# Expert stages: the two rows of routing weights of a pair fetched by one indirect DMA from GpSimd instead of two broadcasts from SyncE

## The chip, the cores and the metric

One core of a Trainium2 chip runs the whole program. The metric is the device time of one execution in microseconds (us); lower is better. The engines are named as the profile names them: PE (TensorE), PEld (its weight loads), DVE (VectorE), ACT (ScalarE), POOL (GpSimd), SP (SyncE). A name with a q (SPq, POOLq) is the sequencer of that engine, which also issues DMAs.

## What is computed

A transformer of two layers on x of shape (2, 1024, 128), each with an attention and a mixture-of-experts block:

```python
x = x + attn_a(layernorm(x))      # 16 heads, all positions
x = x + ffn(layernorm(x))
x = x + attn_b(layernorm(x))      # 16 heads, a window of 32 positions
x = x + ffn(layernorm(x))
# ffn, for T = 2048 tokens of 128 channels, 64 experts of 64 hidden channels:
shared = silu(x @ sg_w.T) * (x @ su_w.T) @ sd_w.T
scores = sigmoid(x @ gate_w.T) + gate_bias
# the best 4 of 8 groups of experts, in them the best 6 experts; their scores normalised to sum 1
comb   = weights (T, 64), zero for the experts not chosen
h      = silu(x @ eg_w) * (x @ eu_w)            # for every expert
routed = einsum('eti,ehi,te->th', h, ed_w, comb)
```

## The kernel before

**Stages.** The program runs in five parts: a start, attention a (`attend_full`), the first expert stage (`experts`, tag M1ex, some 421 to 706 us in the trace), attention b (`attend_banded`), the second expert stage (tag M2ex, some 861 to 1139 us). Between parts stands a barrier over all engines (`end_of_layer`, L65).

**An expert stage.** All 64 experts are computed for all tokens, and the routing weights switch the unwanted ones off. The shared expert counts as two more, so there are 66, in 33 pairs (`PAIRS`); a pair fills the 128 partitions, 64 hidden channels each. The 2048 tokens are two batches of 1024, and a batch is two chunks of 512 columns. The loop counter q runs over 132 steps (`QN`): batch, then pair, then chunk; p = q // 2 counts the pairs of both batches (0 to 65). One step q is:

- PE, `gate_up(q)`: three matmuls of 128x512 into the gate bank and three into the up bank (the inputs are cut in high and low halves of 16 bits, hence three), L1829 to L1836;
- ACT, `silu(q)` (L1886) from PSUM to `sil`;
- DVE, `times_up(q)` (L1930), then `times_weight(q)` (L1940), which multiplies with the row of routing weights in `cb` and writes `hid`, a ring of 3;
- ACT, `high_part(q)` (L1892): the upper 16 bits, `high`;
- POOL, the subtraction that gives `low` (L1993), also a ring of 3. It waits for `high_ready` q+1 and for `down_done` q-2 (the down product of step q-3 is through);
- PE, `down(q)`: three matmuls (L1845, L1846, L1848), issued `LAG` = 3 steps later, behind `gate_up(q+3)`. The third reads `low`.

`times_weight(q)` waits for `low_ready` q-2, since the subtraction of step q-3 reads the same `hid` buffer.

**Work beside.** In the first batch's steps the engines also take one small slice per step of the output projection, norm and routing of the second batch (`before()` in each engine's block); from step 74 on, in the first stage, the norm and the projections of the next attention (`after()`). POOL's share of these is small: a power for the norm (L1393), the subtraction for `xl` (L1499) and one product of the routing (L1505).

**The rings and the queues.** `cb` has 5 buffers (`CB_RING`) of 128x1024 f32: partitions 0 to 63 hold the weights of the pair's first expert for all 1024 tokens of the batch, partitions 64 to 127 those of the second. They come from `comb` in DRAM, 66 rows by 2048 tokens. Pair 0 is the shared expert, filled by a DVE copy (L1961). `wt`, the six matrices of a pair, has 6 buffers. SP issues everything in program order: in each turn p it waits until `cb`'s buffer is free (`hid_ready` of pair p-5), issues the two broadcasts of pair p (`weights`, L1784, 64 partitions each, all read from one row of 4 KB), then waits for `down_done` of pair p-6 and loads the matrices (L1736). In turn 33 it first stores the second batch's `comb` (`store_weights`, L1490), and `weights(33)` waits until that has landed (`comb_stored[1]`). In the first stage turn 52 also issues the eight stores of the next attention's queries and keys (L1670); in the second, SP stores the output.

## Time and profile before

| | us |
|---|---|
| median of 3 runs | 1148.68 |
| lowest, highest | 1146.83, 1162.83 |
| span of the profiled execution | 1143.3 |
| PE busy in it | 1044.1 (91%) |
| DVE busy | 925.3 (81%) |
| ACT busy | 709.0 (62%) |
| POOL busy | 461.7 (40%) |

The span reaches from the first to the last instruction of the profiled execution. No separate time of that execution is given; its span is 5.4 us below the median of the three timed runs, and what lies around the span (launch and end) is taken as those 5.4 us. Busy times leave out waiting and the issuing of DMAs, so a DMA issued by POOL would not appear in POOL's 40%. Matmuls overlap in their pipeline, and the duration of one (some 380 ns) is longer than its share of PE's time.

### The profile page before, as it was taken

Reading aid. Unit: us, or ns where it says so; the run is one execution under the profiler, and the core shown is the slowest. Engines: PE = TensorE matmul, PEld = TensorE weight load, DVE = VectorE, ACT = ScalarE, POOL = GpSimd, SP = SyncE. Lnnn points to the kernel's source line nnn. Section 1 sums busy time; section 2 is a strip of 40 time slices with the busy share of each in tenths; the row PEclk is TensorE's granted clock in tenths of the full one; section 3 lists DMA queues with packets and bytes.
Section 4 is the critical chain, followed back from the end, with each engine's and each line's share of the span. In section 5 each row is a group of like instructions: output and inputs, shape, how many; then the busy total and the mean of one; then the engine's idle time right before and its main releaser. Section 6 shows DMA issues by size and latency. Waiting matters only on the chain. (4 is left out here: it accounts for less than half of the span.)

```text
span 1143.3 us, 18866 instructions
## 1 busy us (share of the span) xinstructions
PE 1044.1 (91%) x6314; PEld 427.5 (37%) x6314; DVE 925.3 (81%) x2139; ACT 709.0 (62%) x1089; POOL 461.7 (40%) x434
## 2 busy tenths in 40 slices
PE   5769999999999979999999998888888999999998
PEld 4212222222222325444444443334444444444443
DVE  8688999999998467889788776877876779877775
ACT  2537778777787765666666664355465566666664
POOL 4116336532100105565564554100113556556554
PEclk9758999999999989999999999679999999999999
DMA  6901302311200126566764873142206667687662
GB/s 207 253 2 28 81 9 72 80 53 28 54 2 1 43 59 170 163 170 174 196 181 140 218 193 81 34 110 59 72 4 172 157 152 188 171 208 193 182 189 57
DMA packets 72185, 131.63 MB, mean 115 GB/s; under 512 B 12680, under 2 KB 47624, under 8 KB 72088
## 3 DMA queue, kind: packets, MB, share of 16 engines
q1 hardware_dynamic: 68704, 120.92, 40.5%
q10 hardware_dynamic: 3384, 9.51, 3.1%
q8 instruction: 50, 0.82, 0.3%
q14 instruction: 47, 0.39, 0.1%
HBM read 115.08 MB, written 14.91 MB: 114 GB/s over the span
## 5 line engine op out<-in xcount | busy, mean ns | idle before, releaser
L421 ACT ACTIVATE Aatt_prob<-Aatt_st 128x1024 f32<-128x1024 f32 x256 | 247.7, 1022 | 66.1 <-PE Aatt_st L315 65.1
L487 DVE TENSOR_REDUCE Aatt_mx<-Aatt_sc 128x1 f32<-128x512 f32 x439 | 273.3, 683 | 10.0 <-PE Aatt_sc L302 9.5
L1993 POOL TENSOR_TENSOR M1ex_low<-M1ex_hid,M1ex_high 128x512 f16<-128x512 f32 x132 | 152.8, 1157 | 136.2 <-ACT M1ex_high L1892 70.1
L1993 POOL TENSOR_TENSOR M2ex_low<-M2ex_hid,M2ex_high 128x512 f16<-128x512 f32 x132 | 152.7, 1157 | 130.8 <-PE M2ex_acc L1848 73.3
L302 PE MATMUL Aatt_sc<-ks,qs 48*128 48x512 bf16 x496 | 152.5, 408 | 29.5 <-DVE Aatt_mx L487 11.8
L1886 ACT ACTIVATE M2ex_sil<-M2ex_ring,unscale 128x512 f32<-128x512 f32 x132 | 90.7, 687 | 95.3 <-PE M2ex_ring L1831 95.1
L1886 ACT ACTIVATE M1ex_sil<-M1ex_ring,unscale 128x512 f32<-128x512 f32 x132 | 90.7, 687 | 89.4 <-PE M1ex_ring L1831 88.9
L327 PE MATMUL Aatt_pv<-Aatt_prob,vg 128*32 128x512 f32 x1024 | 137.9, 611 | 0.6 <-ACT Aatt_prob L421 0.6
L1930 DVE SCALAR_TENSOR_TENSOR M2ex_ring<-M2ex_ring,unscale,M2ex_sil 128x512 f32<-128x512 f32 x132 | 100.0, 757 | 42.0 <-ACT M2ex_sil L1886 38.9
L1930 DVE SCALAR_TENSOR_TENSOR M1ex_ring<-M1ex_ring,unscale,M1ex_sil 128x512 f32<-128x512 f32 x132 | 99.9, 757 | 36.2 <-ACT M1ex_sil L1886 32.9
L302 PEld LDWEIGHTS Aatt_sc<-ks,qs 48*128 48x128 bf16 x496 | 35.9, 94 | 201.1 <-DVE Aatt_mx L487 167.7
L315 PE MATMUL Aatt_st<-qs,ks 51*128 51x512 bf16 x512 | 105.2, 387 | 4.0 <-ACT Aatt_prob L421 2.6
L1940 DVE TENSOR_TENSOR M1ex_hid<-M1ex_ring,M1ex_cb 128x512 f32<-128x512 f32 x132 | 91.3, 692 | 16.2 <-DVE M1ex_ring L1930 0.9
L1940 DVE TENSOR_TENSOR M2ex_hid<-M2ex_ring,M2ex_cb 128x512 f32<-128x512 f32 x132 | 91.3, 692 | 15.9 <-DVE M2ex_ring L1930 0.5
L828 DVE CUSTOM_DVE_ANT_0 Batt_sc<-Batt_sc,mask 128x160 f32<-128x160 f32 (+1 forms) x256 | 75.2, 347 | 25.5 <-PE Batt_sc L658 24.1
L1892 ACT CAST M1ex_high<-M1ex_hid 128x512 f16<-128x512 f32 x132 | 80.6, 610 | 17.9 <-DVE M1ex_hid L1940 15.9
L1892 ACT CAST M2ex_high<-M2ex_hid 128x512 f16<-128x512 f32 x132 | 80.5, 610 | 12.1 <-DVE M2ex_hid L1940 10.4
L787 ACT ACTIVATE Batt_prob<-Batt_st 128x320 f32<-128x320 f32 x128 | 51.1, 436 | 55.3 <-PE Batt_st L728 54.9
L1829 PE MATMUL M1ex_ring<-M_xh,M_wt 128*128 128x512 f16 x132 | 50.5, 383 | 11.0 <-DVE M1ex_hid L1940 5.4
L248 POOL CAST Aatt_mparts<-Aatt_m 128x32 bf16<-128x32 f32 x8 | 2.6, 325 | 140.1 <-DVE Aatt_m L500 140.1
L1829 PE MATMUL M2ex_ring<-M_xh,M_wt 128*128 128x512 f16 x132 | 50.4, 382 | 5.7 <-DVE M2ex_hid L1940 3.4
L1848 PE MATMUL M2ex_acc<-M2ex_low,M_wt 128*128 128x512 f16 x132 | 50.3, 381 | 1.0 <-POOL M2ex_low L1993 1.0
(437 smaller groups left out, 1959.5 us busy)
## 6 DMA issues: line engine op xcount, KB each, us to landing
M1ex_cb<-comb SPq DMA_DIRECT2D x130, 256.0 KB, 4.1
M2ex_cb<-comb SPq DMA_DIRECT2D x130, 256.0 KB, 4.2
M_wt<-wsplit SPq DMA_DIRECT2D x132, 192.0 KB, 4.0
wsplit<-split_cut SPq DMA_DIRECT2D x9, 704.0 KB, 4.5
qs<-stack SPq DMA_DIRECT2D x32, 96.0 KB
ks<-stack SPq DMA_DIRECT2D x30, 96.0 KB
split_raw<-in_wg_dram ACTq DMA_DIRECT2D x3, 704.0 KB, 8.5
split_raw<-in_wu_dram ACTq DMA_DIRECT2D x3, 704.0 KB, 12.0
```

The lines of the kernel that those rows point to most:

```text
L302: mm = pe.matmul(sc_bank(n, i), queries, ks[k][rows, jp, h * CH:(h + 1) * CH], start=True, stop=kind != "excess")
L315: mm = pe.matmul(st[jp][:, half, :], ks[k][rows, jp, kc * P:(kc + 1) * P], qs[k][rows, jp, qh * CH:(qh + 1) * CH], start=True, stop=True)
L327: mm = pe.matmul(pv[32 * j:32 * j + 32, :], vg[k][:, kc, j, :], prob[(2 * s + j % PAIR) % 4][:, j // PAIR, :], start=kc == 0, stop=kc == T ...
L421: act.activation(prob[e % 4][:, :, :].rearrange("p a c -> p (a c)"), st[pr][:, :, :].rearrange("p a c -> p (a c)"), ACT.Exp, scale=SCALE). ...
L487: ins = dve.tensor_reduce(mx[k][:, m, h:h + 1], scores, AX.X, ALU.max)
L828: ins = dve.tensor_tensor_reduce(scores, scores, mask_q[:, first:BAND], -1.0, -BARRED, ALU.add, ALU.min, accum_out=m1[k][:, j, qt:qt + 1])
L1829: pe.matmul(gate(q)[:, :], wt[k][:, 0, :], env.xh[:, cs], start=True, stop=False)
L1886: act.activation(sil[q % 2][:, :], gate(q)[:, :], ACT.Silu, scale=env.unscale[:, 0:1]).then_inc(sil_ready, 1)
L1892: act.copy(high[q % 3][:, :], hid[q % 3][:, :]).then_inc(high_ready, 1)
L1930: dve.scalar_tensor_tensor(up(q)[:, :], up(q)[:, :], env.unscale[:, 1:2], sil[q % 2][:, :], ALU.mult, ALU.mult).then_inc(up_ready, 1)
L1940: dve.tensor_tensor(hid[q % 3][:, :], up(q)[:, :], cb[k][:, c * CH:(c + 1) * CH], ALU.mult).then_inc(hid_ready, 1)
L1993: pool.tensor_tensor(low[q % 3][:, :], hid[q % 3][:, :], high[q % 3][:, :], ALU.subtract).then_inc(low_ready, 1)
```

## The change

The broadcasts leave SP's program. POOL issues, for each pair, one indirect DMA that writes all 128 partitions of the `cb` buffer: a small table `which` of 128x33 integers, made by two `iota` instructions in the start part, says for partition k and pair j which row of `comb` goes there (2j for the lower 64 partitions, 2j+1 for the upper). The table is read as offsets by the DMA. Four of them (pairs 1 to 4) are issued ahead of POOL's loop, the others one in every second step: in step q (odd) for pair q // 2 + 4, ahead of that step's subtraction. Pair 33 is thus issued in step 59, and waits there for `comb_stored[1]`. `comb` becomes two DRAM tensors, one for each batch. One DMA raises the semaphore by 16 where two raised it by 32.

```diff
             pool.wait_ge(made, 14)
+            for e in range(2):
+                pool.iota(env.which[HALF * e:HALF * e + HALF, :], [[2, PAIRS]], base=e, channel_multiplier=0).then_inc(made, 1)
+            pool.wait_ge(made, 16)
             rest_of(norm_of_batch_gpsimd(pool, env, second))
...
         @block.sync
         def _(sp):
-            def weights(p):
-
-                j, b = p % PAIRS, p // PAIRS
-                if j == 0:
-                    sp.wait_ge(env.comb_stored[b], 32)
-                for e in range(2):
-                    sp.dma_start(cb[p % CB_RING][64 * e:64 * e + 64, :],
-                                 env.comb2[j, e:e + 1, b * S:(b + 1) * S].to_broadcast([64, S])).then_inc(cb_in[p % CB_RING], 16)
-
...
-            sp.wait_ge(env.comb_stored[0], 32)
-            for p in range(1, CB_RING):
-                weights(p)
             for p in range(CB_RING, B * PAIRS):
                 sp.wait_ge(hid_ready, 2 * (p - CB_RING) + 2)
                 if p == PAIRS:
                     store_weights(sp, env, q1, 1)
-                weights(p)
                 if p >= WT_RING:
...
                 if c == 0 and p:
-                    dve.wait_ge(cb_in[k], 32 * (p // CB_RING + (k > 0)))
+                    dve.wait_ge(cb_in[k], 16 * (p // CB_RING + (k > 0)))
...
+            def weights(p):
+
+                if p % PAIRS == 0:
+                    pool.wait_ge(env.comb_stored[p // PAIRS], 32)
+                if p >= CB_RING:
+                    pool.wait_ge(hid_ready, 2 * (p - CB_RING) + 2)
+                pool.indirect_dma_start(cb[p % CB_RING][:, :], None, env.comb_rows[p // PAIRS][:, :], bass.IndirectOffsetOnAxis(
+                    ap=env.which[:, p % PAIRS:p % PAIRS + 1].bitcast(U32), axis=0)).then_inc(cb_in[p % CB_RING], 16)
+
             beside, behind = before(), after()
+            pool.wait_ge(env.comb_stored[0], 32)
+            for p in range(1, CB_RING):
+                weights(p)
             for q in range(QN):
+                if q % 2 and CB_RING <= q // 2 + CB_RING - 1 < B * PAIRS:
+                    weights(q // 2 + CB_RING - 1)
                 pool.wait_ge(high_ready, q + 1)
                 if q >= 3:
                     pool.wait_ge(down_done, q - 2)
...
-        env.comb_rows = nc.dram_tensor("comb", [ROWS, B * S], F32).ap()
-        env.comb2 = env.comb_rows.rearrange("(j e) t -> j e t", e=2)
+        env.comb_rows = [nc.dram_tensor(f"comb{b}", [ROWS, S], F32).ap() for b in range(B)]
+        env.which = sb("which_row", [P, PAIRS], I32)
```

## Rows read from the trace of the kernel before

**Rows 1.** The page, busy time of each engine, share of span, instructions.
```profile
PE 1044.1 (91%) x6314; PEld 427.5 (37%) x6314; DVE 925.3 (81%) x2139; ACT 709.0 (62%) x1089; POOL 461.7 (40%) x434
```
**Rows 2.** Windows: stretch, length, busy PE, PEld, DVE, ACT, POOL, clock, DMA share, GB/s.
```profile
430.00:706.00 276.00, 269.60 (x1287) 127.50 (x1284) 219.75 (x391) 170.59 (x284) 158.22 (x136) 1.00 0.67 173
870.00:1139.00 269.00, 265.00 (x1259) 124.25 (x1257) 208.41 (x353) 163.64 (x273) 155.91 (x135) 0.99 0.64 167
...
1000.00:1050.00 50.00, 50.00 (x237) 23.21 (x236) 37.84 (x53) 31.75 (x53) 29.45 (x26) 1.00 0.81 202
```
**Rows 3.** Waits, 421 to 706 us: us in total, times, longest.
```profile
POOL M1ex_low L1993 <- ACT M1ex_high L1892: 70.1, 52, 18.1
POOL M1ex_low L1993 <- PE M1ex_acc L1848: 65.1, 75, 2.1
...
PEld M1ex_ring L1829 <- issue: 11.8, 10, 5.5
PEld M1ex_ring L1829 <- DVE M1ex_hid L1940: 6.4, 10, 2.5
```
**Rows 4.** The page, costliest groups: shapes, count, busy, mean ns, idle before.
```profile
L1993 POOL TENSOR_TENSOR M2ex_low<-M2ex_hid,M2ex_high 128x512 f16<-128x512 f32 x132 | 152.7, 1157 | 130.8 <-PE M2ex_acc L1848 73.3
...
L1930 DVE SCALAR_TENSOR_TENSOR M2ex_ring<-M2ex_ring,unscale,M2ex_sil 128x512 f32<-128x512 f32 x132 | 100.0, 757 | 42.0 <-ACT M2ex_sil L1886 38.9
...
L1940 DVE TENSOR_TENSOR M2ex_hid<-M2ex_ring,M2ex_cb 128x512 f32<-128x512 f32 x132 | 91.3, 692 | 15.9 <-DVE M2ex_ring L1930 0.5
```
**Rows 5.** Timeline, 550 to 557 us (steps 57 to 60): start, duration, instruction, idle before.
```profile
550.55 0.38 PE L1848 MATMUL M1ex_acc<-M1ex_low,M_wt 128*128 128x512 f16 x1
550.94 1.15 POOL L1993 TENSOR_TENSOR M1ex_low<-M1ex_hid,M1ex_high 128x512 f16<-128x512 f32 x1 [0.78 <-PE M1ex_acc L1848]
...
552.72 1.09 SPq L1784 DMA_DIRECT2D M1ex_cb<-comb  x2
552.89 1.16 POOL L1993 TENSOR_TENSOR M1ex_low<-M1ex_hid,M1ex_high 128x512 f16<-128x512 f32 x1 [0.79 <-PE M1ex_acc L1848]
...
554.83 1.16 POOL L1993 TENSOR_TENSOR M1ex_low<-M1ex_hid,M1ex_high 128x512 f16<-128x512 f32 x1 [0.79 <-PE M1ex_acc L1848]
555.17 0.69 DVE L1940 TENSOR_TENSOR M1ex_hid<-M1ex_ring,M1ex_cb 128x512 f32<-128x512 f32 x1
...
556.38 0.38 PE L1848 MATMUL M1ex_acc<-M1ex_low,M_wt 128*128 128x512 f16 x1
```
**Rows 6.** DMA issues on SP by line: issue ns min/median/max; time to landing of L1784.
```profile
L1784 SPq DMA_DIRECT2D M1ex_cb<-comb x130: 444/596/1578, 421.7 to 685.1; - x130
DMA to landing us min/median/max: 3.3/4.1/7.8
...
L1736 SPq DMA_DIRECT2D M_wt<-wsplit x132: 325/584/1316, 373.5 to 1117.0; - x132
```
**Rows 7.** Timeline of the second expert stage's first 11 us.
```profile
860.84 11.43 SPq L1784 DMA_DIRECT2D M2ex_cb<-comb  x11
860.89 0.69 DVE L1961 COPY M2ex_cb<-unscale 128x1024 f32<-128x1024 f32 x1 [7.23 <-PEq L69]
...
866.63 1.16 POOL L1993 TENSOR_TENSOR M2ex_low<-M2ex_hid,M2ex_high 128x512 f16<-128x512 f32 x1 [17.98 <-ACT M2ex_high L1892]
...
869.38 0.69 DVE L1940 TENSOR_TENSOR M2ex_hid<-M2ex_ring,M2ex_cb 128x512 f32<-128x512 f32 x1
```
**Rows 8.** Timeline of DVE: the norm beside the second expert stage.
```profile
911.65 0.17 DVE L1367 TENSOR_TENSOR M2exln_r<-M2exln_r 128x8 f32<-128x8 f32 x1 [1.75 <-POOL M2exln_r L1393]
```
**Rows 9.** Timeline of POOL in the start part.
```profile
10.47 1.95 POOL L983 TENSOR_SCALAR_AFFINE_SELECT mask<-mask 128x320 bf16<-128x320 bf16 x4
...
13.34 0.13 POOL L997 MEMSET fresh_g<- 128x8 bf16 x1
25.88 1.64 POOL L1393 TENSOR_TENSOR startln_r<-startln_ve,minus_half 128x8 f32<-128x8 f32 x1 [12.41 <-DVE startln_ve L1363]
```
**Rows 10.** POOL's groups by line: its only library instruction.
```profile
L1091 POOL PARTITION_ALL_REDUCE split_alltop<-split_top x1 | 0.4, 420 | 5.7 <-issue 5.7
```

More of the change, by code:

```diff
@@ L1489, in store_weights @@
         sp.wait_ge(q.comb_copied, c + 1)
-        sp.dma_start(env.comb_rows[:, b * S + c * CH:b * S + (c + 1) * CH],
+        sp.dma_start(env.comb_rows[b][:, c * CH:(c + 1) * CH],
                      q.combT[:, c * CH:(c + 1) * CH]).then_inc(env.comb_stored[b], 16)
```

## The prediction

> **What bounds the kernel now.** I read the page first: PE is busy 91% of the span, POOL 40% [rows 1]. Since the change touches the two expert stages, the average says little, and I cut those stages into windows. From 1000 to 1050 us PE is busy 50.00 of 50 us; over both stages without their first microseconds it is busy 269.6 of 276 and 265.0 of 269 [rows 2]. So PE sets the pace there, and any transfer or engine that is not later than PE is free. The timeline of four steps gives the pace: the third down matmul of step 54 starts at 550.55, that of step 57, three steps on, at 556.38, so 5.83 / 3 = 1.94 us a step, 3.89 us a pair [rows 5]. Next I asked whether anything waits for what is taken out. The waits of the stage have no line in which DVE waits for `cb`; POOL's own waits, 70 and 65 us, are for ACT and for the down matmuls [rows 3]. The broadcasts land 4.1 us after issue (7.8 at most) [rows 6], and are issued four pairs, some 15 us, ahead. What the change removes is thus hidden already, and the question is what it adds to POOL.
>
> **POOL's room.** A subtraction takes 1.157 us [rows 4], two of them in a pair 2.31 us. In a pair of 3.89 us that leaves 1.57 us, if PE sets the pace. Averaged over both stages: 545 us of window less 158.2 + 155.9 us of busy POOL is 230.9 us, and 61 issues fall in each stage's loop (pairs 5 to 65), so 230.9 / 122 = 1.89 us for each [rows 2]. The mean is higher since some steps carry more side work; that surplus can't be moved to other pairs, because the rings hold only three steps. So the limit for POOL's cost D of one indirect DMA lies at 1.57 us in the dense stretches and 1.89 us over all.
>
> Within that limit the delay itself must be harmless too. In step 59 the DMA would go out when the subtraction of step 58 is over, 552.89 + 1.16 = 554.05. The subtraction of step 59 starts at 554.83 now, so it comes D - 0.78 us late [rows 5]. Who waits for it: the down matmul of its own step, and DVE's write of `hid` three steps later. For the first, `low` of step 57 is done at 552.09 and read at 556.38: 4.3 us of room. For the second, DVE writes `hid` of step 60 at 555.17: 3.1 us of room. A D of up to 0.78 + 3.1 = 3.9 us would pass as a single delay; only the sum over a pair, 1.57 us, binds.
>
> **The part without a row: D.** The trace has no DMA issued by POOL. From below: SP's generator is held 0.58 us by the matrices' load, a 128-partition transfer [rows 6], and POOL's one library instruction is shown with 0.42 us [rows 10]. A software generator isn't likely to beat the first, and I exclude a gain, because POOL issued nothing of the kind before; the low end is 0.4 us. From above: 5.7 us of idle before that library instruction, for which the profile shows no reason [rows 10], and 4.1 us, if POOL were held until the data are there [rows 6]. Between those ends the nearest row is the same work on the other engine: the two broadcasts of a pair, together 128 rows of 4 KB, hold SPq 1.09 us [rows 5]. I take that, D = 1.1 us, with a likely spread of 0.6 to 2.3 us, twice the row. At 1.1 us POOL needs 3.41 of 3.89 us: the steady state costs nothing, and what hides it is PE's pace.
>
> The Trainium skill, on its page "SBUF — State Buffer" (section "A bandwidth-pool intuition that's wrong"), has a rule that speaks against the change: a DMA issued by GpSimd has its descriptors written by that engine through a port that VectorE locks in its two-port modes, and one that takes some 620 ns alone took some 3100 ns beside such a copy. By 3.1 us for each, the sum would be 122 x (3.1 - 1.57) = 187 us. The trace speaks against it here: DVE's two large operations of every step read `ring`, a PSUM bank [rows 4], and POOL's subtraction next to them has a mean of 1157 ns, no instance of it stretched enough to move that mean. The one large copy from SBUF to SBUF, 0.69 us, stands at the stage's start [rows 7], exactly where the first four DMAs go: at most 0.7 us, and covered as below.
>
> **The other edits.** *Four DMAs ahead of the loop.* POOL sits idle for 17.98 us before its first subtraction at 866.63, and the barrier ends at 860.84, when SP starts: 5.8 us for four DMAs, 4.4 us at my D. If that cover is gone (D above 1.45) the first subtraction is late, with over 3 us of room to its readers. DVE first needs `cb` of pair 1 at 869.38; issued at 860.84, it is there at 860.84 + 1.1 + 4.1 = 866.0 [rows 6, 7]. Nothing. *The wait in step 59.* SP's own wait for the stored rows ended at 552.72, when it issued the next broadcast; POOL reaches the wait at 554.05, 1.3 us later [rows 5]. Behind that wait stands the subtraction of step 59, and if the store were late it has 3.1 us more. Nothing, twice. *The wait for `hid_ready`* in each step asks for q - 1, and the subtraction before it already needed step q - 1 finished: no wait. *The norms beside the loop.* DVE waits 1.75 us for POOL's power [rows 8], and PE for DVE up to 2.5 us [rows 3], so here POOL is on the path, three times in the program (two norms in the first stage, one in the second). The DMA stands ahead of the subtraction ahead of the power and makes it D - 0.78 = 0.3 us late: 3 x 0.3 = 1 us; at D = 2.2 it would be 4 us. *The two `iota`.* They write 64x33 integers; four operations of 320 columns take 1.95 us, and POOL idles 12.41 us right behind them [rows 9]. Nothing. *SP* loses 130 issues of 0.6 us in each stage [rows 6] and waits instead. The matrices are issued up to 1 us earlier, with a ring of six pairs ahead: nothing, unless the rival below holds. *DMA traffic* stays 512 KB a pair for `cb`; the engines are 64 to 67% busy [rows 2].
>
> **Sum.** Profiled span 1143.3 + 0 (loop) + 1 (norms) = 1144.3; with the 5.4 us between span and median, 1149.7, say 1150 us.
>
> **Rivals.** *POOL becomes the bound (slower).* The mechanism is D itself: above 1.57 us each pair takes 2.31 + D. At D = 2.2, twice SPq's row, that is 0.6 us a pair. Over 122 pairs at most 74 us, at least (2.2 - 1.89) x 122 = 38 us; I take 60, with the norms' 4 some 1210 us. For it: the offsets must be fetched before a descriptor can be made, and the profile shows how close 1.57 us is to 1.1. Against: only that SPq's row is the nearest. It decides 2% (23 us) from D of about 1.8 us. A far case of the same mechanism, D = 4.1, gives (4.1 - 1.57) x 122 = 309 us, some 1450 us; 4.1 us is a transfer's whole time to landing, which an issuing engine need not sit through, and SPq doesn't.
> *The matrices come sooner (faster).* PE idles with no visible reason before L1829 in the first stage, 11.8 us, 5.5 of them at its start [rows 3]. If the rest of it were a matrix load queued behind broadcasts, the change would give some 6 us back there and as much in the other stage: 1138 us. Against it: loads are issued six pairs ahead.
> *The change doesn't do what it says:* the rows of 4 KB are cut in smaller pieces by the software generator. Then there are more descriptors in a DMA, D grows, and it ends as the slow case.
>
> **How the numbers follow.** A measurement of this kernel can tell some 2% (23 us) from no change. Forecast, D up to 1.8 us: 0.55. POOL the bound, D 1.8 to about 2.6, or cut rows: 0.34. The far case: 0.07. Matrices sooner: 0.04, half of which I allow to pass 2%. So faster 0.02, same 0.57, slower 0.41. The likeliest case's own range is 1140 to 1172. The range must reach into the slow case: up to D = 2.3, (2.3 - 1.57) x 115 = 84 us, 1235; above that lies about 0.13, below 1138 some 0.04.
>
> **What would show it.** Right: in the windows of the expert stages PE stays above 97% busy; POOL's subtraction waits for PE or ACT in the even steps as now, and in the odd steps follows the DMA with no idle time named; no DVE wait for `cb`. Wrong: pairs of more than 3.89 us in 1000 to 1050 us, POOL's subtractions back to back with the DMA (D read off as the gap between the end of an even subtraction and the start of the odd one), PE and DVE waiting for `low`. A D above 1.57 us makes the prediction wrong, and only that can by much.

## The result and the profile after

| | before | after |
|---|---|---|
| median, us | 1149.42 | 1165.47 |
| lowest, highest | 1144.94, 1164.63 | 1153.66, 1169.74 |
| executions | 18 | 18 |

The medians differ by 16 us (1.4%). The estimated ratio is 1.0114, with a 95% interval of 1.0083 to 1.0144 (this estimate, and not the quotient of the medians, stands in the tables below). By the bound of 2% that is no change, but the interval leaves out 1: the kernel is slower, by 16 us in the median where 1 was forecast. The forecast of 1150 us was 15 us too low, inside its range of 1138 to 1235.

The 18 times after the change lie in two groups, 7 from 1153.7 to 1158.2 and 11 from 1164.6 to 1169.7, and the groups differ in the mean clock that PE was granted (0.943 to 0.947 against 0.925 to 0.932). The profiled execution is one of the upper group: 1166.2 us, span 1164.4, so 1.8 us lie around the span. The profile of before has a span of 1143.3 and a clock of 0.948, like its fastest executions. A comparison of the two profiles therefore holds two things at once, and the experiments had to part them.

The page after the change, busy time and the DMA queue (its columns: packets, MB, share of 16 engines):

```profile
PE 1061.5 (91%) x6314; PEld 433.0 (37%) x6314; DVE 933.1 (80%) x2139; ACT 710.8 (61%) x1089; POOL 593.5 (51%) x566
...
q0 software_dynamic: 18720, 68.17, 16.2%
...
L1997 POOL TENSOR_TENSOR M2ex_low<-M2ex_hid,M2ex_high 128x512 f16<-128x512 f32 x132 | 153.9, 1166 | 44.6 <-ACT M2ex_high L1882 32.7
...
L1984 POOL DMA_INDIRECT M2ex_cb<-comb,which_row x65 | 63.9, 983 | 24.1 <-POOLq L69 14.2
L1984 POOL DMA_INDIRECT M1ex_cb<-comb,which_row x65 | 64.9, 999 | 21.8 <-POOLq L69 11.8
```

Against [rows 1] POOL has 132 more instructions, 130 DMAs and two `iota`, and goes from 40% to 51%. Its other work has not stretched: 1166 ns for a subtraction against 1157 [rows 4]. An indirect DMA is shown as work of the engine (POOL, not POOLq), and so does count in POOL's busy share, other than the section on the time before says. It takes 0.98 to 1.00 us in the mean. The queue's 18720 packets are 130 x (128 + 16), and 128 x 130 rows of 4 KB make 68.16 MB: the rows went out whole, so the prediction's third rival, rows cut in smaller pieces, did not occur.

The windows of the expert stages, with the columns of [rows 2]; the fourth is attention b:

```profile
430.00:712.00 282.00, 273.31 (x1295) 128.52 (x1293) 223.09 (x393) 171.76 (x285) 219.70 (x197) 0.99 0.51 170
885.00:1160.00 275.00, 268.82 (x1278) 125.41 (x1276) 215.01 (x362) 168.03 (x278) 219.32 (x198) 1.00 0.49 168
...
1020.00:1070.00 50.00, 50.00 (x237) 23.22 (x236) 37.89 (x54) 31.31 (x53) 41.48 (x39) 1.00 0.58 192
...
716.00:884.00 168.00, 145.81 (x1356) 69.58 (x1357) 116.10 (x653) 74.15 (x180) 19.90 (x48) 0.73 0.19 52
```

In the dense stretch PE is still busy 50.00 of 50 us, and POOL 41.48 instead of 29.45. How a pair looks there, in the timeline of POOL:

```profile
1042.38 1.16 POOL L1997 TENSOR_TENSOR M2ex_low<-M2ex_hid,M2ex_high 128x512 f16<-128x512 f32 x1 [1.22 <-PE M2ex_acc L1838]
1043.68 0.96 POOL L1984 DMA_INDIRECT M2ex_cb<-comb,which_row  x1
1044.65 1.17 POOL L1997 TENSOR_TENSOR M2ex_low<-M2ex_hid,M2ex_high 128x512 f16<-128x512 f32 x1
...
1046.26 1.16 POOL L1997 TENSOR_TENSOR M2ex_low<-M2ex_hid,M2ex_high 128x512 f16<-128x512 f32 x1 [0.44 <-ACT M2ex_high L1882]
```

One subtraction ends at 1042.38 + 1.16 = 1043.54 and the next starts at 1044.65: the DMA costs POOL 1.11 us, gap included. The subtractions ahead of it and behind it still have idle time before them, 1.22 and 0.44 us, in which POOL waits for PE and ACT. POOL is not the bound.

So where are the 21.1 us of span? I cut both traces at DVE's writes of `hid` (steps 0, 66 and 131 of each stage) and at POOL's first copy for attention b, the first thing after the first stage's barrier. The same cut was made for each experiment, and one table serves them all. "Barrier" runs from the last `hid` to that copy; "attention b" from there to the first `hid` of the second stage (so it is longer than the 137 us that the expectations give for it), "tail" from the last `hid` to the end; the last two columns are the clock granted in attention b and the whole span. All in us, the clock as a share of full speed:

| kernel | M1 to 66 | M1 | barrier | attention b | M2 to 66 | M2 | tail | clock | span |
|---|---|---|---|---|---|---|---|---|---|
| before | 141.30 | 277.81 | 6.69 | 154.68 | 143.14 | 269.87 | 8.76 | 0.86 | 1143.3 |
| after | 145.79 | 281.61 | 9.15 | 167.57 | 144.67 | 271.41 | 9.02 | 0.73 | 1164.4 |
| first_only | 144.52 | 280.34 | 9.14 | 156.82 | 143.13 | 269.87 | 8.76 | 0.85 | 1150.9 |
| second_only | 142.73 | 279.24 | 6.83 | 158.39 | 145.60 | 272.33 | 9.03 | 0.84 | 1151.0 |
| onedma | 141.36 | 277.89 | 6.85 | 154.54 | 143.17 | 269.90 | 8.76 | 0.86 | 1144.2 |
| latebarrier | 142.72 | 279.24 | 9.60 | 161.19 | 143.15 | 269.88 | 8.76 | 0.80 | 1154.3 |
| noload | 141.15 | 277.61 | 6.69 | 168.97 | 141.89 | 268.66 | 8.75 | 0.73 | 1155.9 |
| behind | 142.44 | 280.88 | 9.15 | 163.14 | 143.17 | 269.90 | 9.02 | 0.79 | 1157.4 |
| halves | 165.84 | 322.07 | 6.39 | 156.70 | 166.09 | 316.08 | 8.75 | 0.85 | 1236.4 |
| plain_two | 146.03 | 281.93 | 6.38 | 166.04 | 146.33 | 273.07 | 8.74 | 0.76 | 1162.1 |
| second_batch | 142.70 | 278.51 | 6.59 | 163.64 | 141.69 | 268.43 | 8.80 | 0.75 | 1152.8 |
| filled | 144.58 | 280.39 | 9.53 | 156.51 | 145.60 | 272.34 | 9.02 | 0.86 | 1153.8 |
| twice | 141.53 | 278.05 | 6.68 | 161.25 | 143.12 | 269.86 | 8.76 | 0.92 | 1150.8 |
| after_twice | 144.54 | 280.36 | 9.15 | 160.67 | 144.57 | 271.31 | 9.02 | 0.91 | 1156.4 |

The first two lines differ by 3.8 us in the first stage, 2.5 at its barrier, 12.9 in attention b, 1.5 in the second stage and 0.3 behind it, 21.0 together. The second batch of each stage (M1 less "M1 to 66": 136.5 before, 135.8 after; 126.7 in both in the second stage) costs nothing. Whatever the change costs, it costs in the first batch, at the barrier and, most of all, in a stage that the diff does not touch.

**The barrier.** The drain of POOL's queue at the end of each stage (issue ns min/median/max), after; [rows 1 to 10] have no such row, so that of before follows:

```profile
L1752 POOLq DRAIN  x2: 6583/6586/6590, 708.7 to 1156.8; - x2
```
```profile
L1749 POOLq DRAIN  x2: 1256/1256/1256, 704.8 to 1136.0; - x2
```

And the timeline behind it, in the kernel after:

```profile
711.77 0.69 DVE L1937 TENSOR_TENSOR x_res<-x_res,M1ex_side 128x512 f32<-128x512 f32 x1 [0.31 <-PE M1ex_side L1843]
...
716.38 0.40 POOL L612 COPY vg<-vn 128x256 f32<-128x256 f32 x1 [6.52 <-POOLq L69]
...
716.88 0.40 PE L658 MATMUL Batt_sc<-ks,qs 48*128 48x128 bf16 x4 [5.14 <-DVEq L804]
```

DVE, the last worker of the stage, is through at 712.46, and POOL's drain at 708.7 + 6.59 = 715.3. The next stage starts 3.9 us behind DVE; before, DVE's last instruction ended at 708.58 and the copy came at 710.03, 1.45 us behind. At the end of the program SP's store of the output covers nearly all of the same drain, which leaves 0.3 us.

**The first batch.** The norm's wait came as forecast in two of its three places: DVE waits 2.13 and 2.12 us for POOL's power there, against 1.76 and 1.75 before. At the third, the next attention's norm, it waits 2.06 against 2.02. But DVE shows more than that. The routing of the second batch, in the kernel after (timeline of DVE and POOL):

```profile
529.74 1.17 POOL L1997 TENSOR_TENSOR M1ex_low<-M1ex_hid,M1ex_high 128x512 f16<-128x512 f32 x1
530.30 1.89 DVE L1552 TENSOR_TENSOR M1exrt_experts_eq<-M1exrt_masked,M1exrt_experts_top 128x256 bf16<-128x256 f32 x1
530.85 1.05 POOL L1508 TENSOR_TENSOR M1exrt_weighted<-M1exrt_masked,M1exrt_inv 128x512 f32<-128x512 f32 x1
...
533.57 0.42 DVE L1552 TENSOR_TENSOR M1exrt_experts_eq<-M1exrt_masked,M1exrt_experts_top 128x256 bf16<-128x256 f32 x1
```

The same DVE instruction takes 0.42 us alone and 1.89 us when it starts during a POOL instruction: it ends at 532.19, behind the end of the second of two POOL instructions that follow without a gap (531.90). DVE's next write of `hid` comes 3.28 us after the last instead of 1.86. The kernel before pays in this place too, but less: its two comparisons take 0.48 and 1.04 us. So the change doesn't bring these meetings, it makes them longer. The addition to the routing scores is hit too (the groups by line, after, then before):

```profile
L1572 DVE SCALAR_TENSOR_TENSOR M1exrt_sc<-M1exrt_sc,gate_b x1: 1577/1577/1577, 496.9 to 496.9; 128x512 f32<-128x512 f32 x1
```
```profile
L1569 DVE SCALAR_TENSOR_TENSOR M1exrt_sc<-M1exrt_sc,gate_b x1: 810/810/810, 495.1 to 495.1; 128x512 f32<-128x512 f32 x1
```

The Trainium skill has this on its page "SBUF — State Buffer" (section "Who interferes with whom"): a VectorE instruction with two inputs from SBUF and a GpSimd instruction that reads SBUF contend for a port that is an exclusive lock and not a share of bandwidth. The trace agrees, with 0.42 us become 1.89, and adds that one wait can last over two GpSimd instructions. The large DVE operations of each step read `ring` in PSUM [rows 4] and are not touched: 757 and 692 ns, as before.

**Attention b.** The stage takes 12.9 us longer, at a clock of 0.73 instead of 0.86. The window of before that answers to the fourth one above:

```profile
711.00:865.00 154.00, 130.09 (x1357) 62.09 (x1358) 115.72 (x653) 74.03 (x180) 16.76 (x44) 0.86 0.22 58
```

The number of matmuls is the same (1357, 1356), their busy time 130 and 146 us. The granted clock has two levels, 1.2 and 2.4 GHz, and 0.73 is a mean over stretches at either. In every kernel profiled the clock falls to 1.2 GHz in or shortly behind the stretch at the barrier in which PE stands idle (707.85 to 710.53 us before, 711.74 to 716.88 after), and stays there for 27.3 us before and 23.9 us after. So the first low stretch is not what became longer. Up to the next barrier the kernel before has one more, of 13.7 us, and the kernel after three, of 17.1, 17.1 and 27.3 us, the last two from 800.8 and 834.9 us on. The diff changes nothing in this stage.

### The profile page after: what moved, and what is told of

Read it like the earlier page. It is cut to its first block and busy times, and to the rows that moved or that the text cites. A ratio compares the mean times of both kernels' runs of the same rounds, so it can differ in the third digit from the quotient of the medians.

```text
span 1164.4 us, 18861 instructions
## 1 busy us (share of the span) xinstructions
PE 1061.5 (91%) x6314; PEld 433.0 (37%) x6314; DVE 933.1 (80%) x2139; ACT 710.8 (61%) x1089; POOL 593.5 (51%) x566
## 3 DMA queue, kind: packets, MB, share of 16 engines
q0 software_dynamic: 18720, 68.17, 16.2%
## 5 line engine op out<-in xcount | busy, mean ns | idle before, releaser
L1997 POOL TENSOR_TENSOR M2ex_low<-M2ex_hid,M2ex_high 128x512 f16<-128x512 f32 x132 | 153.9, 1166 | 44.6 <-ACT M2ex_high L1882 32.7
L1984 POOL DMA_INDIRECT M2ex_cb<-comb,which_row x65 | 63.9, 983 | 24.1 <-POOLq L69 14.2
L1984 POOL DMA_INDIRECT M1ex_cb<-comb,which_row x65 | 64.9, 999 | 21.8 <-POOLq L69 11.8
## 6 DMA issues: line engine op xcount, KB each, us to landing
split_raw<-in_wu_dram ACTq DMA_DIRECT2D x3, 704.0 KB, 13.7
```

The lines of the kernel that those rows point to most:

```text
L1984: pool.indirect_dma_start(cb[p % CB_RING][:, :], None, env.comb_rows[p // PAIRS][:, :], bass.IndirectOffsetOnAxis(ap=env.which[:, p % PAIR ...
L1997: pool.tensor_tensor(low[q % 3][:, :], hid[q % 3][:, :], high[q % 3][:, :], ALU.subtract).then_inc(low_ready, 1)
```

## The experiments

**1. Which stage, and is it the number of DMAs?** Four kernels. `first_only` and `second_only` are the changed kernel with the DMAs on POOL in one expert stage and SP's broadcasts in the other:

```diff
+        by_pool = not last          # second_only: by_pool = last
...
+                if not by_pool:
+                    weights(p)                  # SP, the two broadcasts
...
-                    dve.wait_ge(cb_in[k], 16 * (p // CB_RING + (k > 0)))
+                    dve.wait_ge(cb_in[k], (16 if by_pool else 32) * (p // CB_RING + (k > 0)))
...
-                if q % 2 and CB_RING <= q // 2 + CB_RING - 1 < B * PAIRS:
+                if by_pool and q % 2 and CB_RING <= q // 2 + CB_RING - 1 < B * PAIRS:
```

`onedma` is the kernel before with one small DMA issued by POOL in each expert stage, for a drain that has something to drain:

```diff
             beside, behind = before(), after()
+            pool.dma_start(tiny[:, :], env.sources["gate"]).then_inc(tiny_in, 16)
```

`latebarrier` is the kernel before with six fills of a `cb` buffer behind POOL's last subtraction of the first stage, so that POOL comes late to the barrier without any DMA:

```diff
+            if not last:
+                for i in range(6):
+                    if i == CB_RING:
+                        pool.wait_ge(idle_set, CB_RING)
+                    pool.memset(cb[i % CB_RING][:, :], 0.0).then_inc(idle_set, 1)
```

> The first expert stage as in the changed kernel, the second as before. Theory A (the loss is local: some 4 us inside the first stage's first batch, some 2.5 us at the barrier behind it, because POOL's drain takes 6.6 us instead of 1.3; attention b's lower clock in the profiled run is drawn by each execution, not caused): profile shows the first stage and the barrier as in the changed kernel, second stage as before, and the fastest runs lie 6 to 7 us above the fastest of before. Theory B (attention b runs at a lower clock because the stage ahead of it used POOL's DMAs): attention b again takes 150 us or more instead of 137, in most executions, and the median lies 15 us or more above before. Theory C (the DMA queue of POOL itself costs something everywhere, stores and loads of other stages included): other stages longer too.

> The second expert stage as in the changed kernel, the first as before. Theory A: 2 us above before (1.5 us inside the stage's first batch, 0.3 us at its end, where SyncE's store of the output covers most of the longer drain). Theory B: the same, since attention b stands ahead of the POOL DMAs; its clock must be that of before. If attention b is slow here too, B falls and the clock is drawn whatever the change.

> The kernel before, and in each expert stage POOL issues one small plain DMA (a 128x64 tile, read by nobody) at the stage's start. If the longer drain of POOL is a fixed price of having used its DMA queue in a block, it is 6.6 us here as well and the barrier behind the first stage comes 2.5 us later: 2.5 to 3 us above before. If it grows with the number of DMAs (69 in a stage), it is near 1.3 us and the time is that of before.

> The kernel before, with six memsets of 128x1024 on POOL (some 0.9 us each) behind its last subtraction of the first stage, so that the barrier comes some 2.5 us later without any POOL DMA. Theory A: 2 to 3 us above before, attention b as before. Theory B in its form 'the later barrier, with PE idle for 5.4 instead of 2.9 us, sends attention b into the lower clock': 10 us or more above before in the median, with attention b at a mean granted clock of 0.75 to 0.8 instead of 0.9.

| kernel | median | lowest, highest (n) | ratio to before, 95% |
|---|---|---|---|
| first_only | 1163.03 | 1152.08, 1165.36 (6) | 1.0122, 1.0081 to 1.0162 |
| second_only | 1151.54 | 1148.60, 1156.23 (12) | 1.0027, 1.0000 to 1.0055 |
| onedma | 1146.61 | 1145.54, 1153.73 (12) | 0.9995, 0.9975 to 1.0015 |
| latebarrier | 1156.05 | 1151.17, 1165.18 (10) | 1.0062, 1.0031 to 1.0094 |

The DMAs of the first stage alone bring as large a loss as the whole change (1.0122 against 1.0114); those of the second alone bring some 3 us (1.0027). `first_only` falls in two groups as the kernel after does (two times at 1152, four from 1161.9 to 1165.4), and its profile is of the lower one: with attention b at 0.85 it has all of the first stage's loss and only 2 of the 12.9 us. Both theories of its expectation are borne out in part: the lowest times lie 8 us above those of before (A forecast 6 to 7), and the median 15.7 us (B: 15 or more). One DMA in a stage (against 65 in the kernel after; the 69 of the expectation was a miscount) costs nothing, and its drain is 1.20 us:

```profile
L1749 POOLq DRAIN  x2: 1197/1200/1202, 705.7 to 1137.0; - x2
```

So the longer drain is not the price of using POOL's queue at all.

`latebarrier` delayed the barrier by 2.9 us (9.60 against 6.69) and cost more than that, 7 us at its lowest (1151.17 against 1144.29) and 8.7 in the median, between the 2 to 3 and the 10 or more of its two theories, with five of its ten times at 1156 to 1157. Of the 11.0 us in its profile 2.9 are the barrier, 1.4 the steps 22 to 26 told of below and 6.5 attention b at a clock of 0.80. A later start of attention b alone can thus go with time beyond the delay itself, but does not produce the upper group in most executions.

The table also shows a second thing that comes and goes. Steps 22 to 26 of a stage take 7.6 us in some profiles (M1 of before, of `first_only` and of `twice`; M2 of `noload` and of the kernel after) and 9.1 or 9.2 in others (M1 of the kernel after and of `second_only`; M2 of before and of `first_only`), with or without POOL's DMAs. What happens there in the longer case, in the windows of the kernel after:

```profile
474.00:478.00 4.00, 1.97 (x6) 0.79 (x7) 3.69 (x9) 1.31 (x2) 2.32 (x3) 0.81 0.41 154
478.00:482.00 4.00, 4.00 (x15) 1.62 (x14) 3.23 (x7) 1.81 (x3) 2.32 (x3) 0.76 0.19 43
```

PE is busy 1.97 of 4 us beside the norm, and the granted clock falls to 0.81 and 0.76, means over one stretch of 3.4 us at 1.2 GHz. What decides it is open: in the same place of before PE is busy 2.31 of 4 us and the clock stays at 1.00. A profile that has this carries 1.2 to 1.5 us more at step 66. Between profiles that agree in it, the DMAs cost 144.52 - 141.30 = 3.2 us up to step 66 of the first stage (`first_only` against before), of which 0.7 come back by step 84, and 144.67 - 141.89 = 2.8 us in the second (after against `noload`). The 3.8 and 1.5 us of the profiled pair are thus 2.5 + 1.3 and 2.7 - 1.2. Other pairs that agree in it give 2.4 us for the first stage (after against `second_only`) and 2.5 (`second_only` against before) to 3.0 (after against `second_batch`) for the second.

Where the loss arises shows step by step. In the second stage of `second_only` against that of before, DVE's write of `hid` falls back by 0.4 us at step 21 (the norm), 0.8 at step 31 (the addition to the scores, 1.57 us instead of 0.81), 0.35 at steps 35 and 36 (the comparisons of the groups), 0.3 at step 41 (the masking of the scores, 0.95 instead of 0.68), and 0.8 at steps 47 and 48 (the two comparisons above, 1.90 and 0.42 instead of 0.49 and 1.04). With rounding and 0.1 us won back at step 24 that is the 2.5 us. All but the norm are DVE instructions that read SBUF alone, the addition, the masking and the two comparisons with two inputs.

**2. Was the removed work worth anything, and does the place of the DMA matter?** `noload` is the kernel before with the broadcasts of 61 pairs in each stage left out, the first four pairs' kept, so DVE multiplies with old rows; neither SP nor POOL issues them:

```diff
                 if p == PAIRS:
                     store_weights(sp, env, q1, 1)
-                weights(p)
+                if p == PAIRS:
+                    sp.wait_ge(env.comb_stored[1], 32)
...
-                if c == 0 and p:
+                if c == 0 and 0 < p < CB_RING:
```

`behind` is the kernel after with the DMA moved behind the subtraction and the side work of its step:

```diff
             for q in range(QN):
-                if q % 2 and CB_RING <= q // 2 + CB_RING - 1 < B * PAIRS:
-                    weights(q // 2 + CB_RING - 1)
...
                 if q >= AFTER:
                     next(behind, None)
+                if q % 2 and CB_RING <= q // 2 + CB_RING - 1 < B * PAIRS:
+                    weights(q // 2 + CB_RING - 1)
```

`halves` cuts each indirect DMA in two, of 128 rows of 2 KB each, for the left and right 512 tokens: twice the instructions and rows, the same bytes. `plain_two` issues SP's two broadcasts from POOL, 64 partitions each, without offsets:

```diff
-                pool.indirect_dma_start(cb[p % CB_RING][:, :], None, env.comb_rows[p // PAIRS][:, :], ...
+                # halves
+                for c in range(2):
+                    pool.indirect_dma_start(cb[p % CB_RING][:, c * CH:(c + 1) * CH], None,
+                        env.comb_rows[p // PAIRS].rearrange("r (c t) -> (r c) t", c=2), ...
...
+                # plain_two
+                for e in range(2):
+                    pool.dma_start(cb[p % CB_RING][64 * e:64 * e + 64, :],
+                        env.comb_rows[b][2 * j + e:2 * j + e + 1, :].to_broadcast([64, S])).then_inc(cb_in[p % CB_RING], 16)
```

> The kernel before, with no transfer of routing weights behind pair 4: cb keeps the rows of the first pairs, so the experts are weighted wrongly; 61 pairs of broadcasts are left out in each stage, and nothing takes their place. It tells what the removed part was worth. Forecast of the prediction: nothing, within 3 us of before, since no engine waited for it. Rival (the matrices come sooner): 6 us or more faster for each stage.

> The changed kernel with the indirect DMA of an odd step issued behind that step's subtraction and side work instead of ahead. If the loss inside the first batch comes from the subtraction and the norm's power being late (0.4 us at the norm, then a lower clock of PE), it is gone or smaller here: 3 to 5 us faster than the changed kernel. If it comes from VectorE's operations on two SBUF tiles meeting POOL at work (1.3 us around step 47 in each stage), it stays about as it is, at other operations.

> The changed kernel with two indirect DMAs a pair, each of 128 rows of 2 KB (one for each half of the tokens), so the same bytes, twice the descriptors and instructions. POOL needs 2.31 + 2 x 1.27 = 4.85 us a pair where PE gives 3.89. If D is per instruction or per descriptor (0.96 us for 128 rows): POOL becomes the bound, up to 0.96 us more for each of 122 pairs, 80 to 115 us above the changed kernel. If D goes by bytes: 0.5 us for each half, and no change.

> The changed kernel with two plain broadcasts of 64 rows from POOL in place of the one indirect DMA: what indirection costs. If D is a fixed price of an instruction: POOL needs 2.31 + 2 x 1.27 us and the time goes up by 80 to 115 us. If it goes by descriptors (64 each) with a small fixed part: 2 x 0.6 us, time within 10 us of the changed kernel.

| kernel | median | lowest, highest (n) | ratio to before, 95% |
|---|---|---|---|
| noload | 1154.04 | 1147.83, 1161.96 (12) | 1.0041, 1.0011 to 1.0070 |
| behind | 1161.48 | 1149.34, 1163.19 (12) | 1.0093, 1.0061 to 1.0125 |
| halves | 1238.67 | 1237.49, 1248.95 (4) | 1.0809, 1.0745 to 1.0873 |
| plain_two | 1153.19 | 1148.74, 1164.05 (10) | 1.0036, 0.9996 to 1.0076 |

`noload`: with nearly all fetches gone from the chip the kernel is no faster. Its first stage is 0.2 us shorter than that of before, its second 1.2, which is the clock of steps 22 to 26. The removed broadcasts were worth nothing in the stages that had them, as forecast; the median is even 4 us above that of before, 1 more than the expectation allowed. And its attention b ran at 0.73 without a single DMA on POOL:

```profile
711.00:880.00 169.00, 148.72 (x1357) 71.28 (x1358) 117.12 (x650) 74.16 (x180) 16.82 (x44) 0.73 0.20 55
```

So the low clock of that stage doesn't need POOL's DMAs. It has low stretches in the same places, too (17.1 and 27.3 us from 795.3 and 829.4 on). It varies from execution to execution of one kernel, and how often it is low differs from kernel to kernel: 8 of the 12 executions of `noload` have a mean clock below 0.940, against 6 of 29 of before in the same comparison.

`behind`: the place of the DMA moves the loss more than it removes it. Ten of twelve times are at 1159 to 1163. The norm is no longer late (DVE waits 1.8 us for the power, as before), but other DVE operations are caught (the comparison `groups_eq` takes 0.82 us instead of the 0.41 of before, the addition to the scores 1.07 instead of 0.81). In the first stage part of the loss comes only behind step 66, and at its end 280.88 us stand against 280.34 of `first_only`. The second stage looks free of loss (269.90 against 269.87), but has the short steps 22 to 26 where before has the long ones; against the short ones of `noload` and `second_batch` (268.66 and 268.43) it loses 1.2 to 1.5 us, half of what the kernel after loses. Which operation meets POOL is a matter of phase.

`halves`: this is the rival "POOL becomes the bound", made on purpose. A window of its first stage, and POOL's timeline there:

```profile
600.00:650.00 50.00, 42.88 (x192) 18.62 (x190) 37.40 (x69) 25.36 (x42) 43.93 (x42) 0.97 0.42 142
```
```profile
602.75 0.97 POOL L1986 DMA_INDIRECT M1ex_cb<-comb,which_row  x1 [0.16 <-issue]
604.02 0.95 POOL L1986 DMA_INDIRECT M1ex_cb<-comb,which_row  x1 [0.30 <-issue]
605.00 1.17 POOL L2000 TENSOR_TENSOR M1ex_low<-M1ex_hid,M1ex_high 128x512 f16<-128x512 f32 x1
```

Each half takes as long as a whole DMA, 0.96 us, at half the bytes, and the second starts 1.27 us after the first. The gaps between POOL's instructions have no releaser but "issue"; the first stage takes 322.07 us, 4.88 a pair instead of 4.2, and PE falls to 42.88 of 50. The cost goes by the rows or the instruction, not by the bytes, and a second microsecond of it is 73 us of median (80 to 115 were expected).

`plain_two`: two plain broadcasts cost POOL 0.53 us each, 1.07 together, about as much as one indirect DMA:

```profile
L1986 POOL DMA_DIRECT2D M1ex_cb<-comb x130 | 69.1, 534 | 15.9 <-POOLq L69 11.5 <-DVE M1ex_hid L1930 2.0 <-DMA comb<-M1exrt_combT 1.8
```

Its expert stages lose as much as those of the kernel after (281.93 and 273.07), so the loss of the first batch is not a matter of indirect DMAs, but its barrier is as early as before, 6.38 us. Its median is 12 us below that of the kernel after, of which the barrier explains some 3; the rest is how often attention b has the low clock.

**3. What makes the drain long, and would PE's idle time at the barrier explain the clock?** `second_batch` fetches pairs 1 to 32 by SP and 33 to 65 by POOL, each with semaphores of its own:

```diff
+        by_pool = lambda p: p >= PAIRS
...
+                if not by_pool(p):
+                    weights(p)                  # SP
```

`filled` is the kernel after with 18 matmuls of no use behind the last of the first stage, into a bank that nobody reads, to keep PE busy through part of the longer barrier. `twice` is the kernel before with the matmul that brings the mask in attention b issued twice, which raises PE's share of that stage:

```diff
             for c in range(2):
                 back(1, c)
+            if not last:                        # filled
+                for _ in range(18):
+                    pe.matmul(bank[2][:, :], wt[0][:, 0, :], env.xh[:, 0:CH], start=True, stop=True)
...
-                        pe.matmul(st[pr][:, :], env.ident16[:, :], mask_k[:, :], start=True, stop=True)
+                        for _ in range(2):      # twice
+                            pe.matmul(st[pr][:, :], env.ident16[:, :], mask_k[:, :], start=True, stop=True)
```

> Both stages: SyncE broadcasts for pairs 1 to 32, POOL's indirect DMAs for pairs 33 to 65 only (33 of 65, in steps without the next batch's routing beside them). If the loss inside the stages belongs to the first batch's side work (3.9 us in the first stage, 1.5 in the second), both stages are as before within 0.5 us: the DMAs themselves hide. The drain of POOL at the block's end was 6.6 us behind 65 indirect DMAs of 128 rows, 3.2 us behind 130, 2.1 us behind 130 plain ones of 64 rows, 1.2 us behind one. If it grows with the number, half of 65 gives some 3.9 us, and the barrier is that of before.

> The changed kernel with 18 matmuls (into a bank that nobody reads any more) on PE behind its last work of the first stage, 3.9 us, so that PE isn't idle while POOL drains. If the idle time at the barrier is what sends attention b into lower clocks, the slow half of the executions (1165 us) goes away and nearly all lie at 1154 to 1157. If not, the two groups stay as they are.

> The kernel before, with the mask product of attention b (128x320, twice in each block of a stage, 128 in all) issued twice: the same values written again. It adds some 128 x 0.13 = 17 us of work at full clock to PE, which is busy 118 of 137 us there only because part of that runs at half clock. If the spread of the executions of every kernel comes from attention b being near the edge at which the clock is granted, more PE activity holds the clock: attention b at 1.0 nearly throughout, the spread smaller and the time not above before, perhaps 3 to 8 us below. If PE is the bound of attention b at full clock as well, it is 10 us or more slower.

| kernel | median | lowest, highest (n) | ratio to before, 95% |
|---|---|---|---|
| second_batch | 1150.95 | 1143.26, 1158.50 (12) | 0.9998, 0.9959 to 1.0037 |
| filled | 1165.92 | 1155.06, 1169.09 (6) | 1.0115, 1.0056 to 1.0174 |
| twice | 1153.29 | 1151.57, 1157.36 (12) | 1.0035, 1.0006 to 1.0065 |

`second_batch` keeps half of the change and costs nothing: its stages take 278.51 and 268.43 us against 277.81 and 269.87, and the differences are those of steps 22 to 26 (long in its first stage, short in its second) and the 0.7 us that come back by step 84. So the DMAs cost nothing in steps without the routing beside them, which points once more to that side work. Its barrier is as early as before, since its drain (706.8 + 3.97 = 710.8) ends within 0.2 us of DVE's last instruction. The drains of the other kernels, each with its own DMAs in a stage (33 indirect; 130 indirect in `halves`; 130 plain in `plain_two`):

```profile
L1752 POOLq DRAIN  x2: 3970/3972/3975, 706.8 to 1145.5; - x2
```
```profile
L1753 POOLq DRAIN  x2: 3233/3238/3242, 749.9 to 1229.1; - x2
```
```profile
L1752 POOLq DRAIN  x2: 2089/2093/2097, 709.3 to 1154.8; - x2
```

Of each, up to 1.2 us is the last subtraction. With 1, 33 and 65 indirect DMAs the drain takes 1.20, 3.97 and 6.59 us, 0.08 us for each DMA. With 130 it is shorter again, so a plain proportion is wrong, and what makes it grow is left open.

`filled` speaks against PE's idle time as what does it. Its extra matmuls ran through the barrier (4.05 us of PE work from 710.75), so that PE idles 1.6 us there, less than the 2.7 of before; its barrier is as late as the one after, and four of its six times are in the upper group. `twice` has a clock of 0.92 in attention b; its window, against that of before:

```profile
711.00:865.00 154.00, 134.07 (x1446) 64.51 (x1447) 114.15 (x650) 69.13 (x174) 17.05 (x45) 0.91 0.19 52
```

Its 12 times span 5.8 us, where the 23 of before in the same comparison span 18.4. The price is the extra PE work, 161.25 us for the stage: the kernel is 3.5 us slower in the median and not the 3 to 8 us faster that the expectation thought possible.

**4. The change without the draw.** `after_twice` is the kernel after with the doubled matmul of `twice` (the same two lines). If attention b's clock is what makes the upper group, the group should disappear.

> The changed kernel with the mask product of attention b issued twice, as in the kernel 'twice' (1151.6 to 1157.4 us, median 1153.3, against executions of the unchanged kernel from 1144 to 1163). If the changed kernel's second group at 1165 us is attention b at half clock and nothing else, that group goes away here too: all executions in a band of some 6 us, with a median 8 us above that of 'twice' (3 to 4 us in the first stage, 2.5 at the barrier, 1.5 in the second stage), 1161. If the change costs attention b something else than clock, the median lies 15 us or more above that of 'twice', or two groups stay 10 us apart.

It took 1159.85 us (1155.81 to 1163.76, 7 executions), 1.0092 of before (1.0056 to 1.0127). The times form one band of 8 us instead of two groups, attention b has a clock of 0.91, and the distance to `twice` is 1159.85 - 1153.29 = 6.6 us by the medians, 4.2 by the lowest, 5.6 by the spans. That is the change's own cost with the clock of attention b out of the way. In the profiles `twice` has the longer steps 22 to 26 in its second stage (143.12 at step 66) and `after_twice` has not, which is 1.2 us more, so 5.6 + 1.2 = 6.8 us.

No kernel tried was faster than the one before by a measurable amount.

## Why the prediction was right, and what it missed

**What bounds the kernel, right.** PE is busy 50.00 of 50 us in the dense stretch in both kernels (over the whole stages 96.9% and 97.8%, the first just under the 97% that the prediction named as its sign), and taking the broadcasts away altogether (`noload`) gained nothing.

**D, the cost of one indirect DMA, right.** 1.1 us was taken from SP's row, and 1.11 us was measured between two subtractions. That the two agree to 0.01 us is luck, since no row tied SP's issue time to POOL's; what the working carried was the spread of 0.6 to 2.3 us. The limit of 1.57 us held: with 1.11 the second batch costs nothing, and with two DMAs (`halves`) a pair takes 4.88 us in the mean, where 2.31 us of subtractions and 2 x 1.27 of DMAs make 4.85. The slow rival's mechanism is real, and only its condition (D above 1.57) did not occur. The far case, POOL held until the data land, is excluded: 4.7 us to landing, 0.96 on the engine.

**The port rule, rightly priced low for the DMA.** In the dense stretch the DMA took 0.96 us beside DVE operations that read PSUM, and no group of the page shows a mean above 1.00. But the DMA is held where it starts during a DVE operation with two inputs in SBUF. The longest is the fourth ahead of the loop of the second stage (timeline of DVE and POOL, kernel after):

```profile
884.56 1.22 DVE L1240 TENSOR_TENSOR M2exo_xb<-x_res,b_bo 128x1024 f32<-128x1024 f32 x1
884.61 1.97 POOL L1984 DMA_INDIRECT M2ex_cb<-comb,which_row  x1 [0.30 <-issue]
```

It ends 0.8 us behind the DVE operation, and so does the same one of the first stage (1.62 us) and each of four others of 1.24 to 1.34 us in that stage; a DMA of `plain_two` that starts 0.1 us ahead of this operation in the first stage keeps its 0.55 us. So the meeting of the two engines goes both ways, and it cost a DMA at most 1 us. The Trainium skill's page "SBUF — State Buffer" (section "A bandwidth-pool intuition that's wrong") has 3.1 us for a DMA starved by a two-port copy; no DMA of this size was seen here.

**Four DMAs ahead of the loop, right.** They took 5.7 us together in the first stage (422.54 to 428.26) and 5.8 in the second, as long as the whole cover of 5.8 and more than the 4.4 forecast, since the first and the fourth were longer than 1.1. The first subtraction of the first stage started right behind, at 428.29, some 0.5 us after its input was ready; no wait of PE for it is shown, and none of DVE for `cb`. **The wait in step 59, the two `iota` and SP: right**, nothing: the `iota` take 0.39 us in idle time.

**Matrices sooner, the faster rival: did not occur.** PE's idle time with no visible reason before its first gate matmuls is 11.4 us now, 11.8 before [rows 3], though SP has nothing but matrices to issue.

**The norms, right in size, and the wrong side of the step.** 0.3 us for each of three was forecast; 0.37 was measured at two and 0.04 at the third. What failed is that the step looked only at who waits for POOL by a semaphore. It took no account of DVE's own instructions with two inputs in SBUF, which stretch while POOL is busy; in the dense stretch POOL is busy 83% of the time instead of 59%. All the side work was given 1 us in the whole program, and that of the first batch cost 2.5 and 2.7 us in the two expert stages, 5.2 together (2.4 to 3.0 in each by other pairs of profiles).

**The end of the block, not in the sum at all.** The list of edits went through the loop, the start and SP, but not to what a DMA on POOL's queue does to the drain behind the loop. It costs 2.5 us at the first barrier and 0.3 at the end, 2.8 together.

**The sum.** 5.2 + 2.8 = 8.0 us should have stood where 1 stood; the lowest times differ by 1153.66 - 1144.94 = 8.7. The rest of the 16 us is the clock of attention b, which the prediction gave no term: the kernel after is in its upper group in 11 of 18 executions, and of the 103 different times of the kernel before over all comparisons only 24 lie 9 us or more above the lowest. A forecast that takes one execution's profile as the kernel has no place for such a term. **The 5.4 us around the span** were also wrong: 1.8 us lie there, and the other 3.6 were the distance of the median from a fast execution. That the sum still came out at the measured median of before is since both were added as one.

**What stays open.** Why the low clock of attention b comes more often with POOL's DMAs in the whole first stage. Executions 9 us or more above their own kernel's lowest time are 11 of 18 for the kernel after, 4 of 6 for `first_only`, 4 of 6 for `filled`, 10 of 12 for `behind` and 4 of 10 for `plain_two`, but none of 12 for `second_only` and `onedma`, 1 of 10 for `latebarrier` and 2 of 12 for `noload`; `second_batch`, whose barrier is early and whose lowest time is as low as that of before, has 5 of 12.

The kernel before itself differs between the comparisons: 3 of 18 beside the kernel after, 3 of 27 beside `first_only` and `latebarrier`, 6 of 29 beside `behind`, `noload` and `plain_two`, but 8 of 23 beside `filled` and `second_batch`. So `second_batch` is no different from before in this, and the share for `filled` is the weakest of the high ones. By the mean clock the picture shifts again: `noload` (8 of 12 below 0.940) and `latebarrier` (5 of 10) have a low clock more often than before (6 of 29 and 4 of 27), without a DMA on POOL. The later barrier may be a part of it (`latebarrier` pays some 4 us more than its delay, up to 1.4 of which can be steps 22 to 26, and `plain_two`, without the delay, has fewer high times than the kernel after); PE's idle time in the barrier seems not to be (`filled`, six executions). That the clock of attention b makes the upper group is shown by `after_twice`; what tips it was not found.

## What to carry to other kernels

Before moving a DMA issue to GpSimd, price three things and not one: the engine's microsecond against its room per iteration, the VectorE instructions with two SBUF operands that will meet a busier GpSimd, and the drain of its queue at the next barrier. Ask first whether the issue that is taken away ever made anyone wait; here it never did, so the change could only cost. And before explaining a difference between two profiles, compare the stages that the diff does not touch: if one of them moved, at another granted clock, that part belongs to the spread of executions until an experiment says otherwise.

## What the runs showed of the hardware

- An indirect DMA of 128 rows holds GpSimd 0.96 to 1.00 us, for rows of 4 KB and of 2 KB alike; with its gap it is 1.11 us between two other instructions, and 1.25 to 1.27 from one DMA to the next. Started during a VectorE operation with two SBUF inputs, it ended 0.8 us behind that operation (1.24 to 1.97 us). A plain broadcast to 64 partitions holds GpSimd 0.53 us. The data of the indirect DMA are there 4.6 to 4.7 us after issue, those of the plain broadcast 4.1 by GpSimd's queue and 4.1 by SyncE's [rows 6].
- The drain of GpSimd's queue at the end of a block grows with the indirect DMAs issued in it: 1.20, 3.97, 6.59 us for 1, 33, 65; but 3.24 us for 130 of half the size and 2.09 us for 130 plain ones of 64 rows.
- A VectorE comparison of 0.42 us with two SBUF inputs took 1.89 us when it started during a GpSimd subtraction, ending only behind two GpSimd instructions in a row; the operations that read PSUM kept their 757 and 692 ns.
- The same code of one stage, with PE busy 84 to 88% of the time, ran at mean clocks from 0.73 to 0.86 in the profiles of different kernels and took 154.5 to 169 us; the mean clock of the whole program varied from 0.924 to 0.951 over executions of the kernel before alone. More PE work of no use raised the clock to 0.91 and brought the range of the times from 18 us to 6, but the median with it was 3.5 us above that without it.
